# A sampled convolution's step: products 0 and 1 added by a transfer, and the next image's sums taken by ScalarE

## What is computed

```python
x = x + dcnv4(gn(x), ...)      # layer 0
x = x + conv_bin(gn(x), ...)   # layer 1: 3x3 convolution of signs

def gn(v):                     # 32 groups of 8 channels, over all pixels of an image
    return (v - mean) / sqrt(var + 1e-5)

def dcnv4(x, ...):
    xdw = depthwise3x3(x) + dw_b
    om = xdw @ om_w + om_b                      # 9 taps x (offset x, offset y, mask), each of 32 groups
    value = x @ vp_w + vp_b
    # each tap samples value bilinearly at its place + offset, times its mask; the sum over 9 taps
    return sampled_sum @ op_w
```

## Time and profile before

| | |
|---|---|
| three runs | 3853.02, 3860.18, 3861.33 us; median 3860.18 |
| profiled execution | 3859.76 us, of which 3858.0 are the span from the first to the last instruction |
| mean granted TensorE clock | 0.987 |
| busy, share of the span | PE 94%, DVE 91%, ACT 59%, POOL 15% |
| DMA queue of POOL (q0) | 28.4% of 16 engines' span, 196.11 MB |
| a step, start to start of its first products on DVE | 101 to 106.5 us in images 1 to 6 |

### The profile page before, as it was taken

One profiled execution on the slowest core, in us unless ns is written; L12 is line 12 of the kernel. 1 busy time (PEld: TensorE's weight loads), 2 busy tenths in 40 slices (PEclk: granted clock), 3 DMA queues, 4 the chain that ended last, 5 costly groups with the idle time before them and its releaser, 6 DMA issues. The chain is left out here.

```text
span 3858.0 us, 90635 instructions
## 1 busy us (share of the span) xinstructions
PE 3628.5 (94%) x37696; PEld 2369.5 (61%) x37696; DVE 3510.0 (91%) x2757; ACT 2286.0 (59%) x4547; POOL 565.0 (15%) x412
## 2 busy tenths in 40 slices
PE   4899999999999999999999999999999999858998
PEld 2566666666666666666666666666666666623333
DVE  4899999999999999999999999989999999948776
ACT  5556665666666665666556666665566666235554
POOL 0011111101111111111111001111111111104444
PEclk9999999999999999999999999999999999979999
DMA  6454565445555555455545555555544554345563
GB/s 177 100 111 102 110 125 132 101 111 116 124 120 109 114 123 115 94 108 127 131 99 119 112 121 114 107 122 131 118 100 97 106 107 94 52 158 199 209 215 147
DMA packets 319939, 470.35 MB, mean 122 GB/s; under 512 B 37244, under 2 KB 242684, under 8 KB 313736
## 3 DMA queue, kind: packets, MB, share of 16 engines
q0 software_dynamic: 94080, 196.11, 28.4%
q1 hardware_dynamic: 224584, 266.07, 23.2%
q10 hardware_dynamic: 832, 2.10, 0.1%
HBM read 262.53 MB, written 67.41 MB: 86 GB/s over the span
## 5 line engine op out<-in xcount | busy, mean ns | idle before, releaser
L1026 DVE TENSOR_TENSOR pv<-val,wsum 128x2048 f32<-128x2048 f32 x800 | 1811.2, 2286 | 21.4 <-ACT xdw L557 14.6
L796 PEld LDWEIGHTS ps_add<-ident,pv 128*128 128x128 f32 x12800 | 1401.2, 142 | 356.0 <-issue 223.7
L796 PE MATMUL ps_add<-ident,pv 128*128 128x128 f32 x12800 | 1527.2, 275 | 70.9 <-DVE pv L1026 62.7
L751 PE MATMUL ps_om<-xdw,omw 128*32 128x256 f32 x13824 | 868.4, 384 | 30.4 <-ACT hat L587 29.4
L585 ACT ACTIVATE hat<-ps_om,omb 128x256 f32<-128x256 f32 x576 | 276.0, 479 | 551.2 <-PE ps_om L751 501.9
L979 DVE TENSOR_TENSOR prod<-hat,mwy 128x1536 f32<-128x1536 f32 (+1 forms) x384 | 526.0, 1397 | 82.9 <-DMA wsum<-prod 61.8
L472 POOL DMA_DIRECT2D wsum<-prod x192 | 226.0, 1254 | 2556.8 <-DVE wsum L979 2556.8
L751 PEld LDWEIGHTS ps_om<-xdw,omw 128*32 128x32 f32 x13824 | 391.2, 109 | 330.2 <-issue 95.5
L589 ACT ACTIVATE msk<-ps_om,omb 128x256 f32<-128x256 f32 x288 | 137.0, 476 | 401.4 <-PE ps_om L751 399.3
L965 DVE TENSOR_TENSOR mwy<-hat,msk 128x768 f32<-128x768 f32 x288 | 274.4, 953 | 94.3 <-ACT hat L599 94.3
L722 PE MATMUL ps_bg<-tri,diag 128*32 128x512 f32 x3024 | 346.5, 592 | 11.9 <-ACT tri L551 11.9
(11 more groups left out here) (134 smaller groups left out, 2622.7 us busy)
## 6 DMA issues: line engine op xcount, KB each, us to landing
wsum<-prod POOLq DMA_DIRECT2D x160, 768.0 KB, 7.1
tri<-in_x_dram SPq DMA_DIRECT2D x725, 128.0 KB, 2.9
win<-in_x_dram SPq DMA_DIRECT2D x144, 256.0 KB, 3.6
x<-xres SPq DMA_DIRECT2D x128, 256.0 KB, 5.1
xres<-in_x_dram POOLq DMA_DIRECT2D x124, 256.0 KB, 8.4
out_dram<-c_x SPq DMA_DIRECT2D x31, 1024.0 KB, 4.5
c_x<-x SPq DMA_DIRECT2D x30, 1024.0 KB, 5.3
c_box<-box_d SPq DMA_DIRECT2D x16, 1024.0 KB, 7.4
```

Source lines behind the costliest of these rows:

```text
L751: mm = nc.tensor.matmul(ps_om[G * q:G * q + G, (par + i) % 2, 0:TOK], omw[:, h, comp, :], xdw[:, j % 2, h, q, :], start=h == 0, stop=h == ...
L796: mm = nc.tensor.matmul(ps_add[:, tb, c, :], pv[:, (j + uv) % PBUF, c, P * tb:P * tb + P], consts["ident"][:, :], start=uv == 0 and c % 4 ...
L1026: nc.vector.tensor_tensor(pv[:, (j + uv) % PBUF, :, :].rearrange("p c (r w) -> p c r w", w=W), val[:, :, SR * j + u:SR * j + u + SR, v:v + ...
```

## The change

Three edits. First, product 0 is no longer added by PE: when product 1 is made, POOL issues one SBUF-to-SBUF transfer that adds product 0's buffer into product 1's (`add_pair`), and PE adds 24 buffers a step instead of 25. PE's adds of a step begin in slot 5, in the order 2, 1, 3. DVE's product 4, which overwrites product 0, waits for the transfer. Second, the sums over the next image's x are taken by ACT, in place, as sums of x minus a pivot (the first value of each channel) and of its square; DVE turns them into mean and variance. Third, the small chain on these sums begins in slot 1 in place of slot 0, and PE's group means stand in slots 2 and 3 in place of 1 and 3.

```diff
 SAMPLED = 4
+PAIRED = {1: 0}
+PAIRS = list(PAIRED)
+ADDS_AT = [(13, 14, 15), (16, 17, 18), (19, 20, 21), (22, 23, 24), (), (2, 1, 3), (4, 5, 6), (7, 8, 9), (10, 11, 12)]
+ADDED = [uv for k in (4, 5, 6, 7, 8, 0, 1, 2, 3) for uv in ADDS_AT[k]]
+ADDS = len(ADDED)
 SENT_TAPS = (1, 2, 3, 6, 7)
...
-    return dw(0) + only(means, "mean", (0, 0)) + dw(1) + dw(2) + only(means, "mean", (1, 1)) + dw(3) + values(0) + only(not first, "back", range(4)) + values(1) \
+    return dw(0) + dw(1) + only(means, "mean", (0, 0)) + dw(2) + only(means, "mean", (1, 1)) + dw(3) + values(0) + only(not first, "back", range(4)) + values(1) \
         + only(not first, "project", range(4)) + values(2) + values(3)
...
         gx_tri = sb("gx_tri", [KROWS, CB, 2, CH])
-        bs1 = sb("bs1", [P, CH, HW // 512, 6])
+        pivot = sb("pivot", [P, CH])
+        x_sums = sb("x_sums", [P, 2, CH, 2])
         mv1 = sb("mv1", [P, CH, 2])
...
         pv_full, add_done, add_out = sem("pv_full"), sem("add_done"), sem("add_out")
+        pair_added = sem("pair_added")
         xres_added, stats2 = sem("xres_added"), sem("stats2")
...
         x_ahead = [sem("x_ahead0"), sem("x_ahead1")]
-        sums_made, gx_step = sem("sums_made"), sem("gx_step")
+        sums_made, gx_step, centred = sem("sums_made"), sem("gx_step"), sem("centred")
         gx_root = sem("gx_root")
-        GX_STEPS = 11
+        GX_STEPS = 13
         x2_stored, over_done, aggr2 = sem("x2_stored"), sem("over_done"), sem("aggr2")
...
         DW_AT = [0, 1, 2, 3]
-        MEANS_AT = [1, 3]
-        SCALES_AT = [0, 2, 4, 6]
+        MEANS_AT = [2, 3]
+        SCALES_AT = [1, 2, 4, 6]
         ROOT_AT = 5
...
+                def add_pair(n, j, uv):
+
+                    s = STEPS * n + j
+                    pool.wait_ge(pv_full, SHIFTS * s + uv + 1)
+                    at_least(pool, pair_added, 16 * (len(PAIRS) * s + PAIRS.index(uv)))
+                    nc.gpsimd.dma_start(pv[:, (j + uv) % PBUF, :, :], pv[:, (j + PAIRED[uv]) % PBUF, :, :],
+                                        accum_op=ALU.add).then_inc(pair_added, 16)
+
                 for n in range(NI):
...
                         for k in SENT_TAPS:
-                            if k == 6 and j < CH and n < NI - 1:
-                                load_ahead(n, j, 0, "back3")
+                            if k == 6:
+                                add_pair(n, j, 1)
+                                if j < CH and n < NI - 1:
+                                    load_ahead(n, j, 0, "back3")
                             add_products(n, j, k)
...
-                    act.wait_ge(add_done, SHIFTS * (s + 1))
+                    act.wait_ge(add_done, ADDS * (s + 1))
                     for tb in range(TB):
...
                         .then_inc(bg_free, 2)
+
+                def sums_ahead(n, j, half):
+
+                    act.wait_ge(x_ahead[half], 16 * (CH * n + j + 1))
+                    i = 3 * (CH * n + j)
+                    if half == 0:
+                        nc.scalar.activation(pivot[:, j:j + 1], ahead[half][:, 0:1], ACT.Copy, scale=-1.0).then_inc(centred, 1)
+                        act.wait_ge(centred, i + 1)
+                    nc.scalar.activation(ahead[half], ahead[half], ACT.Identity, bias=pivot[:, j:j + 1],
+                                         accum_out=x_sums[:, half, j, 0:1]).then_inc(centred, 1)
+                    act.wait_ge(centred, i + 2 + half)
+                    nc.scalar.activation(ahead[half], ahead[half], ACT.Square, accum_out=x_sums[:, half, j, 1:2]).then_inc(sums_made, 1)
...
                         if k == ROOT_AT and has_means(n, j, NI):
-                            act.wait_ge(gx_step, GX_STEPS * n + 9)
+                            act.wait_ge(gx_step, GX_STEPS * n + 11)
                             nc.scalar.activation(var1[:, :], var1[:, :], ACT.Sqrt).then_inc(gx_root, 1)
                         if k == BACK_AT and not first:
-                            if j in (1, 2) and has_next(n):
-                                act.wait_ge(sums_made, CH * CH * n + CH * j)
                             summed(s - 1)
...
                             normalise(n1, j1, 1)
+                        if k == AHEAD_AT and j < CH and has_next(n):
+                            sums_ahead(n, j, 0)
+                        if k == 0 and j in (1, 2) and has_next(n):
+                            sums_ahead(n, j - 1, 1)
                         if k == 8 and more:
...
-                    pe.wait_ge(gx_step, GX_STEPS * n + (4, 8)[i])
+                    pe.wait_ge(gx_step, GX_STEPS * n + (6, 10)[i])
                     pe.wait_ge(bg_free, unit(n, j, f"mean{i}", NI))
...
                 def add(s, j, uv):
-                    pe.wait_ge(pv_full, SHIFTS * s + uv + 1)
-                    if uv == 0:
+                    if uv in PAIRED:
+                        pe.wait_ge(pair_added, 16 * (len(PAIRS) * s + PAIRS.index(uv) + 1))
+                    else:
+                        pe.wait_ge(pv_full, SHIFTS * s + uv + 1)
+                    if uv == ADDED[0]:
                         at_least(pe, add_out, s)
...
                             mm = nc.tensor.matmul(ps_add[:, tb, c, :], pv[:, (j + uv) % PBUF, c, P * tb:P * tb + P],
-                                                  consts["ident"][:, :], start=uv == 0 and c % 4 == 0,
-                                                  stop=uv == SHIFTS - 1, is_transpose=True, skip_group_check=True)
+                                                  consts["ident"][:, :], start=uv == ADDED[0] and c % 4 == 0,
+                                                  stop=uv == ADDED[-1], is_transpose=True, skip_group_check=True)
                     mm.then_inc(add_done, 1)
...
-                    def add_next(k, i):
-                        if k < SAMPLED and not first:
-                            add(s - 1, j - 1, SAMPLES_AT[k][i])
-                        elif k >= SAMPLED and i < len(SAMPLES_AT[k]):
-                            add(s, j, SAMPLES_AT[k][i])
+                    def add_next(k, early):
+
+                        before = [uv for uv in ADDS_AT[k][:1] if uv not in PAIRED]
+                        for uv in before if early else ADDS_AT[k][len(before):]:
+                            if k >= SAMPLED:
+                                add(s, j, uv)
+                            elif not first:
+                                add(s - 1, j - 1, uv)
...
                             offsets(*ahead_of, 1)
-                        add_next(k, 0)
+                        add_next(k, True)
                         if ahead_of:
...
                                     project(u, *place(f"project{u}"), unit(n, j, "back3", NI))
-                        add_next(k, 1)
-                        add_next(k, 2)
+                        add_next(k, False)
...
                 for k in range(SAMPLED):
-                    for uv in SAMPLES_AT[k]:
+                    for uv in ADDS_AT[k]:
                         add(STEPS * NI - 1, STEPS - 1, uv)
...
-                def sums_ahead(n, j, half):
-
-                    dve.wait_ge(x_ahead[half], 16 * (CH * n + j + 1))
-                    for i in range(HW // 1024):
-                        last = nc.vector.bn_stats(bs1[:, j, HW // 1024 * half + i, :], ahead[half][:, 512 * i:512 * i + 512])
-                    last.then_inc(sums_made, 1)
-
                 def scales_ahead(n, j, part):
...
-                        for h in range(CH):
-                            nc.vector.bn_aggr(mv1[:, h, :], bs1[:, h, :, :]).then_inc(gx_step, 1)
-                        dve.wait_ge(gx_step, GX_STEPS * n + 1 + CH)
-                        after(3, nc.vector.tensor_copy(mean1[:, :], mv1[:, :, 0]))
+                        after(1, nc.vector.tensor_tensor(mv1[:, :, :], x_sums[:, 0, :, :], x_sums[:, 1, :, :], ALU.add))
+                        after(2, nc.vector.tensor_scalar(mv1[:, :, :], mv1[:, :, :], 1.0 / HW, None, ALU.mult))
+                        after(3, nc.vector.tensor_tensor(var1[:, :], mv1[:, :, 0], mv1[:, :, 0], ALU.mult))
+                        after(4, nc.vector.tensor_tensor(mv1[:, :, 1], mv1[:, :, 1], var1[:, :], ALU.subtract))
+                        after(5, nc.vector.tensor_tensor(mean1[:, :], mv1[:, :, 0], pivot[:, :], ALU.subtract))
                     elif part == 1:
...
                         dve.wait_ge(bg_free, unit(n, j, "mean0", NI) + 2)
-                        after(4, nc.vector.tensor_tensor(mean1[:, :], mean1[:, :], gm, ALU.subtract))
-                        after(5, nc.vector.tensor_tensor(mean1[:, :], mean1[:, :], mean1[:, :], ALU.mult))
-                        after(6, nc.vector.tensor_tensor(var1[:, :], mv1[:, :, 1], mean1[:, :], ALU.add))
+                        after(6, nc.vector.tensor_tensor(mean1[:, :], mean1[:, :], gm, ALU.subtract))
+                        after(7, nc.vector.tensor_tensor(mean1[:, :], mean1[:, :], mean1[:, :], ALU.mult))
```

(22 more changed lines are left out.)

## The result

The changed kernel takes 3808.28 us (median of 4 runs, 3804.91 to 3813.15) against 3858.2 us for the kernel before (median of four runs, the three above and one more); the ratio is 0.9869, with a 95% interval of 0.9856 to 0.9881: 50 us or 1.3% less. The forecast was 3808. The sum came out to the digit, but by luck: its two terms did not, and their errors cancelled.

The account below looks back on a forecast made before the run. PE was taken to set the time, interrupted by DVE about 5.7 us an image. From 3859.8 us, 28 for the pair and 24 for the statistics came off: 3808 us, range 3780 to 3845.

Parts of the forecast that it names:

- 28 us for the pair: Removing one PE add a step, with product 0 added into product 1 by a transfer, was to save 28 us.
- 24 for the statistics: Moving 28 blocks of next-image sums from DVE to ACT was to save 3.5 us an image, seven images: 24 us.
- So 0.9 us a step, for 31 steps: 28 us: Slot 4 without its add: PE gains 0.9 us, not 1.9, as its third offset product then waits for ACT's hat.
- There DVE waits for hats a slot later anyhow, so I count nothing: Late slot 5: DVE's product 5 needs PE's add of product 1, a stop up to about 3 us, priced at nothing.
- Left over: 5.7 - 6.2 + 2.7 = 2.2 us: PE's remaining wait for DVE products an image: 5.7 now, DVE 6.2 shorter, PE 2.7 shorter over three steps.
- the re-exposed transfer at steps 0 and 1 only: Without statistics ahead of slot 8's products, 3.7 of 9.9 us an image come back as DMA waits; 6.2 net.
- Rival (b): Transfer waits grow by what the statistics leave, PE stops for products as often; only 28 us remain, 3832 us; chance 0.22.
- ScalarE's block: Pivot, centring and squaring passes on ACT in slots 7 and 0: 5.2 us (4.8 to 5.9), room 5.1; counted 0.
- rival (c): ACT's block exceeds its room and delays hats and offset products; with table loads for squaring, 3884 us; chance 0.10.
- The transfer: Product 0 into product 1, 1 MB: 9.4 us taken, bound 13.5, against 13.0 us until product 4 overwrites product 0.
- Rival (d): The pair's transfer lands late and DVE stops at product 4 every step; at 14.6 us, 3860 us; chance 0.08.
- "Nothing" for the group means: Starting the chain in slot 1 and group means in slots 2 and 3 was to change nothing in time.

Follow-up runs that it names:

- third pass: The changed kernel with an extra ScalarE pass copying the squares onto themselves in each of the 28 blocks: 3808.89 us; on the fastest kernel (3764.76 us), 3783.19 us.

## Why the prediction was right, and where it was not

**The time, direction and size** were right: 3808.3 against 3808. The terms were 28 us for the pair and 24 for the statistics. Measured: 8 alone for the pair, 50 alone for the statistics with the later group means, and 0 for the pair on top. That the sum met the time was luck.

**"So 0.9 us a step, for 31 steps: 28 us"** failed as a term of the sum. Its first half held: 0.86 us in slot 4, the rest a wait for a hat of 1.26 us, which vanished when the add of slot 4 was kept. What failed is to count it in time. It counts only while PE sets the time, and with the pair DVE does, in the first three steps of an image. With product 10 moved, the kernels with and without the pair differ by 3803.4 - 3783.3 = 20 us in favour of the pair; so most of the 28 was there.

**"There DVE waits for hats a slot later anyhow, so I count nothing"** is the step that took it away. The wait of product 5 for PE's add of product 1 did replace the wait for hats. But the wait for hats stood between tap 7's products and tap 8's, where it also covered the transfer `wsum<-prod`; the new one stands before tap 7's products and covers nothing. The fourth step of an image shows it, in the kernel before (a wait for a hat, and tap 8's products without one) and in the changed kernel (behind the 3.57 us for PE's add, above):

```profile
1696.66 0.96 DVE L965 TENSOR_TENSOR mwy<-hat,msk 128x768 f32<-128x768 f32 x1 [3.17 <-ACT hat L599]
...
1702.35 2.35 DVE L979 TENSOR_TENSOR prod<-hat,mwy 128x1536 f32<-128x1536 f32 x2
```

```profile
1674.84 2.36 DVE L1009 TENSOR_TENSOR prod<-hat,mwy 128x1536 f32<-128x1536 f32 x2 [1.47 <-DMA wsum<-prod]
```

In this image DVE waits for tap 7's transfer in all four steps, 7.5 us; with the statistics alone it does in two, 3.2 us. Over the stretch that is 96.4 us against 64.6. I had reckoned the re-exposed transfer at steps 0 and 1 only, behind the removed statistics. Rival (b), at 0.22, named growing waits for the transfer, but laid them to the removed statistics. They were the pair's: with the statistics alone the waits are 64.6 us (60.5 before, over the same stretch), with the pair alone 78.8. So the transfers took the pair's gain, and not the statistics', which (b) would have lost.

**"Left over: 5.7 - 6.2 + 2.7 = 2.2 us"** an image of waits for `pv`: 3.3 were found (23.2/7), because DVE was held by the transfer as above. The statistics' term of 24 us was too small for another reason: I priced a stop of PE at its idle time. On top of the pair, where the term was reckoned, the statistics brought 43 us (3851.2 to 3808.3). Over the whole execution PE's stops for `pv` fell by 27 us (71.8 to 44.7), about the term, but its waits ahead of the group means fell by 5 as well, and it was busy 9.3 us less (3575.3 to 3566.0), with the lower granted clock behind such stops gone. Alone the statistics brought 50 us: 39 of stops for `pv`, and 10.2 of busy time, of which 6.5 lie behind the four stops with a lower clock; what made the last 4 isn't shown.

**ScalarE's block** was put at 5.2 us with bounds of 4.8 and 5.9; it was 4.3, below the lower bound, because ACT's waits on itself cost next to nothing, an accumulator read put off the next instruction by some 0.1 us only, and the second pass was shorter. The third pass showed that the room has an edge, nearer 5.6 than 5.1 us. The slower rival (c) fell: there is no table load but the one of before, and ACT's block stayed inside its room. The Trainium skill's rule on adds and multiplies (ScalarE: Activation LUTs, Rules for kernel authors) agrees with the rows on engine time, 4.3 us against 2.5, but not on what the edit is worth: moved against the rule, the statistics gained 50 us, because DVE was the late engine and ACT had room.

**The transfer** landed 7.6 us after issue; 9.4 was the nearest row, 13.5 the bound. Rival (d) fell, with about 5 us of slack shown.

**"Nothing" for the group means** is about right as an edit, but it hides that the sums on ACT gain nothing without it: with the chain back in slot 0 the kernel is 51 us slower.

## What to carry to other kernels

When two engines are both nearly the bound, price an edit by who is late in that stretch, and test edits one by one: here one brought everything, the other 8 us alone, nothing beside it, and 20 once a third was in. A wait that "replaces another anyhow" is free only if nothing else was hidden under the old one; look at what lies between the two places. A stop of PE can cost more than its idle time; look at the granted clock behind it. And a cost that leaves the time unchanged may still be there: PE's waits for ScalarE rose by 19 us unseen, and came out in full when DVE stopped being late.

## What the runs showed of the hardware

An accumulating SBUF-to-SBUF transfer of 1 MB as 128 rows of 8 KB landed 7.6 us after its issue and some 7.9 us after its producer, against 9.4 us from the producer to the next use for the same size in two transfers of shorter rows. ACT passes over 128 x 2048 float32 in SBUF took 2.02 us with a bias per partition and 1.92 us without, plus 0.1 us net for the accumulator read, and a wait on its own last result about 0.03 us in this block; behind `gn_tri` in the same traces such a wait is 0.2 us, and why they differ isn't shown. Behind a stop of TensorE of 2.1 us or more the granted clock fell from full to half in some places and not in others: in 4 of 13 before, in all 7 stops (up to 4.7 us each) with the group means early. At half, 32 matmuls of 256 columns took 3.61 us, at the full clock 1.93.
